# Attention row sums: accumulators inside the ring of exponentials, and two matmul sets per unit instead of four

## The reference

```python
h = _ada_ln(x, cond, Wln1, bln1)
q, k, v = heads(h @ Wq + bq), heads(h @ Wk + bk), heads(h @ Wv + bv)   # 16 heads of 32
scores = einsum('bhqd,bhkd->bhqk', q, k) / sqrt(32)
attn = softmax(scores, axis=-1)
x = x + einsum('bhqk,bhkd->bhqd', attn, v) @ Wo + bo
h = _ada_ln(x, cond, Wln2, bln2)
x = x + gelu(h @ W1 + b1) @ W2 + b2
# second layer: graph attention over the first 20 positions, not touched
```

## Time and profile before

| | |
|---|---|
| median of three runs | 3227.49 us |
| the profiled execution | 3228.51 us, its span 3227.1 us |
| phase 2, from first to last row sum but one | 398.19 to 1891.98 us |
| PE busy over the span | 3179.6 us (99%) |
| POOL busy over the span | 1405.7 us (44%) |

### The profile page before, as it was taken

How to read it: one execution, slowest core, us unless ns; L and a number is a source line. 1 busy time by engine, 2 the same in 40 slices (tenths; PEclk the granted TensorE clock), 3 DMA queues, 4 the chain that set the end, 5 groups by cost and what they waited for, 6 DMA issues and landing times.

```text
span 3227.1 us, 44281 instructions
## 1 busy us (share of the span) xinstructions
PE 3179.6 (99%) x16890; PEld 2178.7 (68%) x16890; DVE 2156.4 (67%) x3537; ACT 1388.7 (43%) x2703; POOL 1405.7 (44%) x656
## 2 busy tenths in 40 slices
PE   8999999999999999999999998899999999999999
PEld 7887655555555555555555546688888888778888
DVE  4557888888888888888888886433333332236766
ACT  2221566666666666666666672221111111112332
POOL 0000487877877778778787754200000001002222
PEclk9999999999999999999999999999999999999999
DMA  6684787877878878778787667511101112201221
GB/s 200 200 241 134 183 211 178 197 191 184 205 178 185 200 187 201 180 181 202 193 186 191 165 168 244 171 61 40 39 3 37 40 40 81 79 29 68 75 75 54
DMA packets 170667, 458.10 MB, mean 142 GB/s; under 512 B 18636, under 2 KB 60748, under 8 KB 137911
## 3 DMA queue, kind: packets, MB, share of 16 engines
q0 software_dynamic: 32496, 235.68, 31.5%
q1 hardware_dynamic: 136183, 214.07, 22.0%
q10 hardware_dynamic: 1776, 5.51, 0.7%
HBM read 143.51 MB, written 75.50 MB: 68 GB/s over the span
## 4 chain that ended last, share of the span: by engine, by line
PE 95%; DVE 2%; DMA 2%; ACT 0%; issue 0%; SPq 0%; POOL 0%; DVEq 0%; ACTq 0%; POOLq 0%
PE ps L368 16%; PE ps L654 15%; PE ps L666 15%; PE ps L1162 11%; PE ps L1149 11%; PE ps L444 5%; PE ps L1696 4%; PE ps L672 3%; PE ps L448 3%; PE ps L1709 3%; PE ps L1730 1%; DMA ao<-ao_d 1%; PE ps L1525 1%; PE ps L140 1%; PE ps L1721 1%; PE ps L1179 1%
## 5 line engine op out<-in xcount | busy, mean ns | idle before, releaser
L381 DVE TENSOR_REDUCE nmp<-ps 128x1 f32<-128x512 f32 x1966 | 1200.1, 681 | 157.6 <-PE ps L368 156.6
L732 ACT ACTIVATE pt<-ps 128x512 f32<-128x512 f32 x2048 | 1030.9, 628 | 508.3 <-PE ps L654 508.3
L836 POOL TENSOR_TENSOR pacc<-pacc,pt 128x2048 f32<-128x2048 f32 x186 | 876.1, 4710 | 37.9 <-ACT pt L732 31.8
L654 PE MATMUL ps<-qs,ks 128*128 128x512 f32 x2048 | 809.9, 399 | 0.4 <-ACT pt L732 0.4
L368 PE MATMUL ps<-ks,qs 96*128 96x512 f32 x1966 | 803.9, 409 | 0.1
L368 PEld LDWEIGHTS ps<-ks,qs 96*128 96x128 f32 x1966 | 372.5, 189 | 265.9 <-DVE nmp L381 167.9
L666 PE MATMUL ps<-pt,vq 128*32 128x512 f32 x4096 | 492.5, 598 | 0.0
L654 PEld LDWEIGHTS ps<-qs,ks 128*128 128x128 f32 x2048 | 388.9, 190 | 93.3 <-ACT pt L732 16.6
L1149 PE MATMUL ps<-hpb,w 128*128 128x512 f32 x1536 | 382.3, 398 | 3.4 <-DMA x_d<-x 3.4
L1162 PE MATMUL ps<-w,gp 128*128 128x512 f32 x1536 | 380.5, 396 | 2.3 <-DVE gp L1298 2.3
L1162 PEld LDWEIGHTS ps<-w,gp 128*128 128x128 f32 x1536 | 289.4, 188 | 71.6 <-DVE gp L1298 2.7
(11 more groups left out here) (175 smaller groups left out, 3202.4 us busy)
## 6 DMA issues: line engine op xcount, KB each, us to landing
accd<-pt POOLq DMA_DIRECT2D x222, 1024.0 KB, 8.6
qk_d<-st SPq DMA_DIRECT2D x128, 256.0 KB, 2.9
qs<-qk_d SPq DMA_DIRECT2D x87, 256.0 KB, 6.9
ks<-qk_d SPq DMA_DIRECT2D x42, 512.0 KB, 6.9
xina<-in_x SPq DMA_DIRECT2D x8, 1024.0 KB, 6.6
v_d<-vst SPq DMA_DIRECT2D x32, 256.0 KB, 2.5
vq<-v_d SPq DMA_DIRECT2D x8, 1024.0 KB, 8.4
ao_d<-accs SPq DMA_DIRECT2D x32, 256.0 KB, 6.0
```

The costliest lines, as they stand in the source:

```text
L381: dve.tensor_reduce(nmp[:, n // 4, n % 4:n % 4 + 1], ps[:, ring.bank["max", u], :], AX.X, ALU.max, negate=True).then_inc(s_mr, 1)
L654: pe.matmul(ps[:, score_bank(n), :], ksb[w % 2][:, hh, 128 * kt:128 * kt + 128], qsb[:, v % 3, hh, :], start=True, stop=True).then_inc(s_s ...
L732: act.activation(pt[:, g % 8, hh, :], ps[:, score_bank(n), :], ACT.Exp, scale=SCALE).then_inc(s_exp, 1)
L836: pool.tensor_tensor(pacc[:, :, :], first, pt[:, g % 8, :, :], ALU.add).then_inc(s_add, 1)
```

## The change

The first three exponentials of a unit (tiles 0, 1, 2) are no longer copied or added anywhere: they lie in slots of their own, and the later tiles are added onto them. There are two sets of these three slots, for even and odd units (`exp_slot`), and a ring of six slots for tiles 3 to 15. `accd` and `pacc` are gone, the second buffer for v too, so that the memory is the same.

- Tiles 3, 7, 11 are added onto accumulator 1, tiles 5, 9, 13 onto accumulator 2, all by adding DMAs. Tiles 4, 6, 8, 10, 12, 14, 15 are added onto accumulator 0 by POOL, and an eighth POOL addition puts accumulator 2 onto accumulator 0.
- `pe_sums` has two ones sets (accumulators 1 and 0) and runs at the end of block 2 of the next unit, not of block 0. In the last unit it keeps four.
- The reciprocal is cut into four pieces of 128 columns in blocks 0, 1, 2 (one, one, two); `dve_sums` is at the start of block 3; `pool_values` comes after tile 5, not 2; the store in block 4, not 3.
- v is loaded in four parts, each when the values have used the part that it replaces.
- Wo's staging buffer moves, and the load of a third residual tile waits until Wo is split.

```diff
-ADD_DMA = (1, 2, 4, 6, 8, 10, 12)
-ADD_POOL = (0, 3, 5, 7, 9, 11, 13, 14)
-ADD_PE = (15,)
-LAST_DMA = (1, 2, 5, 6, 10)
-LAST_DVE = (0, 3, 4, 7, 8, 9, 11, 12, 13, 14)
+ACCS = 3
+RING = 6
+ADD_DMA = ((3, 7, 11), (5, 9, 13))
+ADD_POOL = (4, 6, 8, 10, 12, 14, 15)
+LAST_DMA = ((5, 10), (6,))
+LAST_DVE = (3, 4, 7, 8, 9, 11, 12, 13, 14)
+LAST_PE = (15,)
...
+def exp_slot(g):
+    v, kt = divmod(g, 16)
+    if kt < ACCS:
+        return (ACCS + RING) * (v % 2) + kt
+    return ACCS + ((16 - ACCS) * v + kt - ACCS) % RING
+
+def slot_before(g):
+    n = 16 - ACCS
+    i = n * (g // 16) + g % 16 - ACCS - RING
+    return 16 * (i // n) + i % n + ACCS if i >= 0 else None
...
         def pe_sums(v):
...
+            last = v == NU - 1
             pe_bank_free(("sums", v))
             pe.wait_ge(s_on, 1)
-            for kt in ADD_PE:
-                pe_ones(bank, pt[:, (16 * v + kt) % 8, :, :], kt == ADD_PE[0], False)
-            pe.wait_ge(s_dma[1], dma_count(v, dma_tiles(v)[-2]))
-            pe_ones(bank, accd[:, 1, :, :], False, False)
-            pe.wait_ge(s_add, add_count(v, added_tiles(v)[-1]))
-            pe_ones(bank, pacc[:, :, :], False, False)
-            pe.wait_ge(s_dma[0], dma_count(v, dma_tiles(v)[-1]))
-            pe_ones(bank, accd[:, 0, :, :], False, True).then_inc(s_end, 1)
+            if last:
...
+            pe.wait_ge(s_dma[0], dma_count(v, 0, dma_tiles(v, 0)[-1]))
+            pe_ones(bank, accumulator(v, 1), not last, False)
+            pe.wait_ge(s_add, add_count(v, added_tiles(v)[-1]) + (0 if last else 1))
+            pe_ones(bank, accumulator(v, 0), False, True).then_inc(s_end, 1)
...
-                if f == 0 and v:
+                if f == 2 and v:
                     pe_sums(v - 1)
...
         def act_exp(g, hh):
...
+            if hh == 0 and kt < ACCS:
+                if v >= 2:
+                    act.wait_ge(s_end, v - 1)
+            elif hh == 0 and slot_before(g) is not None:
+                before = slot_before(g)
+                ev, ekt = divmod(before, 16)
+                act.wait_ge(s_pv, before + 1)
+                if ekt in added_tiles(ev):
                     act.wait_ge(s_add, add_count(ev, ekt))
                 else:
-                    act.wait_ge(s_end, ev + 1)
+                    d = 0 if ekt in dma_tiles(ev, 0) else 1
+                    act.wait_ge(s_dma[d], dma_count(ev, d, ekt))
...
-                if f == 0 and v >= 2:
-                    dve_recip(v - 2)
+                if v >= 2 and f < 3:
+                    dve_recip(v - 2, ((0,), (1,), (2, 3))[f])
...
+                for d in range(2):
+                    if kt in dma_tiles(v, d):
+                        pool.wait_ge(s_exp, 4 * g + 4)
+                        if kt == dma_tiles(v, d)[0]:
+                            pool.wait_ge(s_pv, 16 * v + 2 + d)
+                        else:
+                            pool.wait_ge(s_dma[d], dma_count(v, d, kt) - 16)
+                        pool.dma_start(accumulator(v, 1 + d), pt[:, exp_slot(g), :, :],
+                                       accum_op=ALU.add).then_inc(s_dma[d], 16)
+                if v < NU - 1 and kt in ADD_POOL:
...
+                if v < NU - 1 and kt == 15:
+                    pool.wait_ge(s_dma[1], dma_count(v, 1, dma_tiles(v, 1)[-1]))
+                    pool.wait_ge(s_add, add_count(v, 15))
+                    pool.tensor_tensor(accumulator(v, 0), accumulator(v, 0), accumulator(v, 2), ALU.add).then_inc(s_add, 1)
-                if kt == 2 and v >= 2:
+                if kt == 5 and v >= 2:
                     pool_values(v - 2)
...
+                if v + 1 < NU and c == NCH - 1 and f in (3, 5, 7):
+                    sp.wait_ge(s_pv, 2 * p - 2)
+                    sp_load_v(w, (f - 3) // 2)
+                if v and c == 0 and f == 1:
+                    sp.wait_ge(s_pv, 16 * v)
+                    sp_load_v(w - 1, 3)
```

More of the change, by code:

```diff
@@ L242, in program @@
         ksb[1] = take("ks1", [128, 4, S], F32R)
[L243 to L246, removed]
+        vq = take("vq", [128, S // 128, 128])
+        pt = take("pt", [128, 2 * ACCS + RING, 4, CH])
         cursor[0] += 2048
@@ L252, in program @@
         assert chain_end <= top - 32768
-        wtmpo = place("wtmpo", [128, NK, D], after_q + 32768)
+        wtmpo = place("wtmpo", [128, NK, D], top - 24576)
         wo = place("wo", [128, 2, NK, D], top - 16384, F32R)
-        s_vq = [sem(f"s_vq{i}") for i in range(2)]
+        s_vq = [sem(f"s_vq{i}") for i in range(4)]
         s_ao = sem("s_ao")
@@ L599, in sp_qkv @@
                         sp.wait_ge(fa.s_turn, NK * NC8)
-                        sp_load_v(0)
+                        for i in range(4):
+                            sp_load_v(0, i)
                     if j == 8 and ci + 2 < NC8:
@@ L755, in dve_sums, with dve_recip @@
             dve.tensor_copy(accs[:, v % 2, :], ps[:, ring.bank["sums", v], :]).then_inc(s_accs, 1)
-        def dve_recip(v):
+        def dve_recip(v, parts=range(4)):
             dve.wait_ge(s_accs, v + 1)
-            dve.reciprocal(accs[:, v % 2, :], accs[:, v % 2, :]).then_inc(s_rec, 1)
+            for q in parts:
+                dve.reciprocal(accs[:, v % 2, 128 * q:128 * q + 128], accs[:, v % 2, 128 * q:128 * q + 128]).then_inc(s_rec, 1)
         def dve_add(kt):
@@ L764, in dve_add @@
             dve.wait_ge(s_exp, 4 * (16 * v + kt) + 4)
[L765 to L771 removed]
+            if kt == LAST_DVE[0]:
+                dve.wait_ge(s_pv, 16 * v + 1)
+            dve.wait_ge(s_add, add_count(v, kt) - 1)
+            dve.tensor_tensor(accumulator(v, 0), accumulator(v, 0), pt[:, exp_slot(16 * v + kt), :, :],
+                              ALU.add).then_inc(s_add, 1)
         def dve_split_wo(k):
@@ L785, in dve_attention @@
                     dve_split_wo(f + 1)
-                if f == 1 and v:
+                if f == 3 and v:
                     dve_sums(v - 1)
@@ L833, in pool_attention @@
+                if v < NU - 1 and kt in ADD_POOL:
+                    pool.wait_ge(s_exp, 4 * g + 4)
+                    if kt == ADD_POOL[0]:
+                        pool.wait_ge(s_pv, 16 * v + 1)
                     else:
                         pool.wait_ge(s_add, add_count(v, kt) - 1)
-                        first = pacc[:, :, :]
-                    pool.tensor_tensor(pacc[:, :, :], first, pt[:, g % 8, :, :], ALU.add).then_inc(s_add, 1)
-                if kt == 2 and v >= 2:
+                    pool.tensor_tensor(accumulator(v, 0), accumulator(v, 0), pt[:, exp_slot(g), :, :],
+                                       ALU.add).then_inc(s_add, 1)
@@ L859, in sp_attention @@
                     load_q(sp, v + 2)
-                if f == 3 and v >= 2:
+                if f == 4 and v >= 2:
                     sp_store_ao(v - 2)
```

85 lines of the change are left out of this document (31 added, 54 removed).

## The result

| | before | after |
|---|---|---|
| median, us (lowest to highest) | 3228.66 (3221.78 to 3232.45) | 3178.47 (3171.64 to 3180.60) |
| profiled execution, us | 3228.51 | 3179.57 |
| its span, us, and mean granted clock | 3227.1, 0.991 | 3178.2, 0.989 |
| first maximum of phase 2, us | 347.2 | 350.6 |
| first to last maximum, us | 1526.2 | 1474.9 |

The ratio is 0.9843, 95% interval 0.982 to 0.9866. The forecast was 3175, with 3168 to 3198 as its range. The last four lines of the table split the span: +3.4 - 51.3 + 1.7 - 2.7 = -48.9 us. The forecast's 53.2 us are -51.5 in the second of these four (30 row sums) and -1.7 in the third (the 31st), and nothing in the first and the last.

A forecast was written before the change was run, and what follows sets the result against it. PE was taken to bound phase 2, busy throughout and alone in its chain of waits. 3228.5 - 53.2 + 0 = 3175.3 us, 3174.3 against the median; with a small share of bounded costs 3175, range 3168 to 3198.

The forecast's parts named there:

- What goes: Phase 2 row sums on PE: two of four ones sets go in each of 31 units, 0.858 us each, saving 53.2 us.
- POOL: POOL's list per unit: 41.6 of 48.07 us; last addition ends 10.8 us into the next unit, 6.6 us to spare.
- The ring of six: ACT's slots for tiles 3 to 15: adding DMAs may take 12.8 to 16.9 us to land; cost taken as 0.
- DVE: Reciprocal pieces in blocks 0 to 2: 0.9 us each, bounds 0.84 and 1.12, fitting DVE's idle time; cost 0.
- the estimate of 0.2: DVE's fixed SBUF read time: three more reciprocal pieces cost 3 x 0.06 = 0.2 us per unit, inside the idle time.
- The last unit: Final unit of phase 2, keeping four ones sets: POOL's late additions may hold DVE; bounds 0 and 5 us, taken as 0.
- the case of which the prediction said that the trace shows nothing: Last unit: a DVE addition held by the port lock during a POOL addition; would put the cost at the upper bound, 5 us.
- Start of phase 2 and the phases behind it: Span before phase 2's first maximum and after its last ones sets: the forecast put nothing of its 53.2 us there.
- A: Late ring slots in units loading k and q: landings of 14 us cost 16 to 32 us, 3191 to 3207; chance 0.14.
- B: DVE loses its play in phase 2: reciprocal pieces of 1.3 us cost PE 0.4 us per unit, 12 us, 3187; chance 0.06.
- C: Adding DMAs become phase 2's bound: landings of 15.0 us make units net 1.9 us longer, 59 us, 3287; chance 0.04.
- D: Last unit costs its upper bound of 5 us, from DVE held by POOL's additions: 3180 us; chance 0.06.

The follow-up runs named there:

- The experiment with four sets: Changed kernel with each of its two ones sets of a unit run twice in all units but the last: 3232.26 us, ratio 1.0001.
- the kernel with both edits: Changed kernel plus own semaphore for DVE's last-unit additions, `pool_values` behind tile 6's DMA there, and SP's phase 3 loads held until its block 2: 3178.61 us, ratio 0.9833.
- the kernel with DVE's own semaphore: Changed kernel with a separate semaphore for DVE's last-unit additions and `pool_values` behind tile 6's DMA there: 3176.74 us, ratio 0.9852.

## Why the prediction was right, and where it was off

- *What goes* (53.2 us). Right. Steady part: 30 row sums x 1.715 = 51.45, measured 51.3. The experiment with four sets takes exactly this away again.
- *POOL*. Said: last addition 10.8 us into the unit, measured 11.2. The 0.4 us are the pitch of 4.7 between additions with nothing between them, which the earlier trace rows do not show (where an issue follows, the pitch is 4.56 in those rows, not 4.57). It did not matter with 6 us to spare.
- *The ring of six*. Right at 0: the longest landing was 13.4 us, the median 8.5. No DMA whose slot is reused in the steady part came later than its allowance, since ACT never waited for one. A ring of five, with about 2 us less for each, cost 2.5 us between the first and the last maximum, so the six slots have more to spare than 12.8 us against a longest landing of 13.4 suggest.
- *DVE*. Said 0.9 us per piece and no cost. A piece is 0.94 us, and 0.99 from start to start before a reduction; two are 1.75. Pieces in all 0.99 + 1.00 + 1.75 = 3.74 us per unit against 3.26 for the whole (1210.09 to 1213.35 in that kernel), 0.48 more, where the estimate of 0.2 was made with the 58 cycles of the table in the Trainium skill's page "VectorE: DVE Perf Modes", section on the TRN2 errata. The same section says below its table that the measured fixed term is about 150 cycles and not 58; by that three more pieces are an estimated 3 x 0.16 = 0.47 us. The runs agree with the 150 and not with the 58 that the prediction took. PE lost nothing by it.
- *The last unit* (0, bounds 0 and 5). This is the step that was mis-sized: 3.4 us. The prediction expected the held work to be "short and comes early". What it named as the cause, DVE held out of memory by POOL's three additions, is not what happened: DVE waited 15.42 us on a semaphore. `s_add` counts POOL's join like any addition, so DVE's first addition of the last unit, which needs no accumulator of unit 30, waits for the join; the diff showed this and I had not read it. The join waited for a DMA that took 13.4 us while phase 3's loads ran. Removing both gives 45.84 us (shown). The landing of tile 13's DMA in unit 30 is 13.3 to 13.5 us in five profiles with the early loads and at most 7.9 in the one with the later loads; that they slow it by sharing the DMA engines is the likely reading, but was not measured. Held block by block against the kernel with both edits, the last unit of the changed kernel is 0.26 us longer in the block with the sums, 2.31 in the block of PE's one wait and 0.61 in the block ahead of the output projection, 3.1 in all.
- The lock was there all the same, where the semaphore did not hide it. In the kernel with DVE's own semaphore, POOL's join, begun 0.8 us after a DVE addition, took 5.91 us instead of 4.58, and the cast queued behind it 4.77 instead of 0.41. With the later loads DVE's first addition of the last unit, begun 2.4 us into POOL's join, took 4.33 us instead of 2.29: it ended 2.15 us behind the join, about its own length. That is the case of which the prediction said that the trace shows nothing. The Trainium skill, "SBUF — State Buffer", section on the two separate sides, says that a DVE operation with two SBUF inputs takes part in this lock; the runs agree.
- *Start of phase 2 and the phases behind it* (0). Measured +3.4 and -2.7. The first goes with the granted clock; of the second I know no more than that no instruction there was changed. But the same part took 1295.5 and 1297.0 us in the two repeats of the changed kernel, so that a difference of 2.7 us in it says nothing. That the two nearly cancel is luck. The steady part is right to 0.2 us, and what is left of the distance between forecast and result is the last unit.
- *Rivals*. A: no wait of ACT for a DMA between 450 and 1750 us. B: no wait of PE for DVE. C: landings were shorter than before in the median, 8.5 against 9.3. D: happened, at 3.4 us of its 5, by another mechanism.

## What to carry to other kernels

Where the chain of waits holds one engine alone, work removed from that engine comes back at its full measured pitch, as long as each helper's list for one period, added up with start-to-start pitches of exactly that order, stays below the new period; and the period can be shortened only to the next list. The closer such a list comes to the period, the less a pitch measured with idle time around it can be trusted: with none left, POOL's list took 48.2 us where the pitches had given 46.2. A result that comes late is cheap if its consumer is moved and not the producer sped up: a join that ends 11.2 us into the unit cost nothing at block 2 and 6.8 us per unit at block 0. And before costing the ends of a loop (first and last period) list what every waited-for count includes: an increment added to a shared counter delays all who count past it.

## What the runs showed of the hardware

- A short wait of PE can cost more than itself. After 4.45 us the granted clock was 0.75 over the next 10 us; after 1.36 us it was 0.66 over 5 us, between the levels of 1.2 and 2.4 GHz. But of 29 waits of 1.31 to 1.37 us at the same place of the kernel with the undivided reciprocal, ten were followed by slow values (2.7 to 3.3 us to the next block) and nineteen by values at full speed (1.85). The one stall of 2.07 us in the changed kernel was followed by values at 1.92 us, so without a loss, while in its first repeat a wait of 2.06 us at the same place was followed by values of 3.36 us and a clock of 0.66. The price of such a wait is thus not fixed even for one kernel, and its length alone does not tell it.
- POOL's addition of 128x2048 numbers: 4.5 to 4.6 us from start to start when a DMA issue follows, 4.7 when another addition does that waits for it, and single ones of 5.4 where POOL had no idle time left.
- DVE's reciprocal from SBUF to SBUF on 128 partitions: 0.94 us for 128 columns, 3.34 for 512, 0.16 us more for each further piece.
- The landing of a 1 MB adding DMA went with SP's loads: 7.6 to 7.9 us without, 13.4 with six loads issued between 1830.9 and 1837.6 us, around its own issue at 1835.93, and 13.3 to 13.5 in four other profiles with the same loads.
